# Values of the next batch moved into the delta rule's substitution, buffers laid out anew, slices in another order

## What is computed

```python
x = L0_attn_x                                             # 8 x 512 x 128
xn = layernorm(x)
x = x + L0_attn(xn) * silu(L0_ffn(xn))
xn = layernorm(x)
x = x + L1_attn(xn) * silu(L1_ffn(xn))

def L0_ffn(x):                       # 8 experts, the top 2 for each token
    h = silu(a) * g; weighted sum of the experts' outputs
def L0_attn(x, Wq, Wk, Wv, Wo):      # 16 heads, keys of 8, values of 64
    v = (x @ Wv).reshape(B, T, HEADS, D_V).transpose(0, 2, 1, 3)
    attn = softmax(where(causal, -inf, q @ k.T / scale))
    return (attn @ v) @ Wo
def L1_attn(hidden):                 # 4 heads of 32: delta rule in chunks of 32
    q, k, v = silu(causal conv(hidden @ W))
    attn = -strictly_lower(kb @ k.T)
    for i in range(1, c):            # the substitution: rows of the triangle, one after the other
        attn[..., i, :i] += attn[..., i, :] @ attn[..., :, :i]
    u, w = (attn + I) @ v, (attn + I) @ kb
    scan over chunks: u_new = u - w @ S; o = q @ S + lower(q @ k.T) @ u_new; S += k.T @ u_new
    mix o with an exponential average, normalise by its mean square, @ Wo
def L1_ffn(x):                       # two layers of windowed attention, then gelu gates
    x = x + local_attention(rotary(l2norm(q)), rotary(l2norm(k)), v) @ wo
    x = x + (a * gelu(g)) @ w2
```

## Time and profile before

| | us |
|---|---|
| median of 3 runs | 2367.35 |
| lowest and highest | 2362.2, 2369.82 |
| the profiled execution | 2383.33 |
| its span, first to last instruction | 2381.5 |
| busy in the span: PE, DVE, ACT, POOL | 1810.0, 1384.0, 1313.1, 537.8 |
| granted clock of PE, mean | 0.85 |

### The profile page before, as it was taken

The page is one execution under the profiler, slowest core; times in us unless marked ns, Lnnn a source line. Parts: engine busy times, 40 slices in busy tenths (PEclk is TensorE's granted clock), DMA queues, the critical chain, the costliest instruction groups (busy, mean ns, idle before and its releaser), DMA issues.

```text
span 2381.5 us, 54180 instructions
## 1 busy us (share of the span) xinstructions
PE 1810.0 (76%) x22372; PEld 1114.9 (47%) x22372; DVE 1384.0 (58%) x3033; ACT 1313.1 (55%) x3546; POOL 537.8 (23%) x597
## 2 busy tenths in 40 slices
PE   4587567886788676887778777986788686986877
PEld 3244234455454444455444544455444444455435
DVE  7633447375655647375755657474756657464653
ACT  1465337672576538662676448662676448661533
POOL 1222022130503022130503032120503032220330
PEclk9789677897789878897789877996889777996999
DMA  8323440003100200003100220003200220001000
GB/s 247 108 80 106 88 109 17 2 17 60 30 3 17 55 20 18 2 17 60 30 3 16 55 20 18 2 17 60 30 3 16 55 20 18 2 18 19 16 1 21
DMA packets 130210, 88.91 MB, mean 37 GB/s; under 512 B 75426, under 2 KB 120908, under 8 KB 126892
## 3 DMA queue, kind: packets, MB, share of 16 engines
q1 hardware_dynamic: 124332, 64.47, 11.4%
q10 hardware_dynamic: 2560, 14.68, 2.7%
q0 software_dynamic: 3072, 6.30, 2.2%
HBM read 41.77 MB, written 28.97 MB: 30 GB/s over the span
## 4 chain that ended last, share of the span: by engine, by line
PE 43%; ACT 19%; DVE 16%; issue 13%; POOL 6%; DMA 2%; SPq 1%; another core or an unknown queue 0%; DVEq 0%; POOLq 0%; ACTq 0%
ACT work_a L809 6%; PE PS L1318 4%; PE PS L599 4%; ACT area_b L1513 3%; PE PS L1396 3%; PE PS L1427 3%; POOL area_b L1698 3%; PE PS L1345 2%; ACT work_a L829 2%; PE PS L571 2%; PE PS L609 2%; PE PS L507 2%; PE PS L1438 2%; PE PS L755 2%; DVE work_a L947 2%
## 5 line engine op out<-in xcount | busy, mean ns | idle before, releaser
L809 ACT ACTIVATE work_a<-PS,work_a 128x512 bf16<-128x512 f32 (+3 forms) x512 | 266.8, 553 | 84.5 <-DVE work_a L947 80.8
L1698 POOL TENSOR_TENSOR area_b<-area_b,tables 128x256 f32<-128x256 f32 x256 | 207.9, 832 | 383.9 <-DVE area_b L1606 383.7
L947 DVE TENSOR_REDUCE work_a<-PS 128x2 f32<-128x1024 f32 (+3 forms) x256 | 200.1, 819 | 80.5 <-PE PS L484 76.6
L829 ACT ACTIVATE work_a<-PS 128x1024 f32<-128x1024 f32 (+1 forms) x192 | 169.5, 883 | 131.5 <-PE PS L484 128.8
L1513 ACT ACTIVATE area_b<-PS,neg_max 128x128 f32<-128x128 f32 x512 | 183.1, 388 | 38.5 <-DVE neg_max L1619 38.4
L1318 PE MATMUL PS<-wqkv,area_b 128*128 128x512 f32 x384 | 193.5, 636 | 7.2 <-DVE area_b L1606 6.5
L599 PE MATMUL PS<-work_a 128*64 128x512 f32 (+3 forms) x1024 | 183.1, 458 | 0.0
L1712 POOL TENSOR_TENSOR rstd_b<-var_eps_b,minus_half 128x4 f32<-128x4 f32 x16 | 16.4, 1027 | 667.0 <-DVE var_eps_b L119 667.0
L1345 PE MATMUL PS<-area_b 64*64 64x128 f32 (+1 forms) x2048 | 150.5, 293 | 17.8 <-ACT area_b L1513 12.0
L537 PE MATMUL PS<-work_a 64*128 64x512 bf16 (+3 forms) x512 | 82.6, 368 | 84.4 <-ACT work_a L809 75.1
L1345 PEld LDWEIGHTS PS<-area_b 64*64 64x64 f32 x2048 | 121.0, 148 | 51.9 <-issue 26.6
(11 more groups left out here) (310 smaller groups left out, 4161.8 us busy)
## 6 DMA issues: line engine op xcount, KB each, us to landing
work_a<-stack_d SPq DMA_DIRECT2D x32, 512.0 KB, 8.9
stack_d<-area_b SPq DMA_DIRECT2D x48, 192.0 KB, 3.1
v_back<-area_b ACTq DMA_DIRECT2D x16, 512.0 KB, 5.7
v_back<-area_b ACTq DMA_DIRECT2D x16, 384.0 KB, 3.7
stack_d<-area_b SPq DMA_DIRECT2D x32, 128.0 KB, 2.6
area_b<-in_L_attn_x_dram SPq DMA_DIRECT2D x4, 512.0 KB, 6.7
stack_d<-work_a SPq DMA_DIRECT2D x4, 512.0 KB, 7.2
work_a<-xnT_d SPq DMA_DIRECT2D x8, 256.0 KB, 3.2
```

The costliest lines, as they stand in the source:

```text
L809: nc.scalar.activation(dump0[:, n % 2 * T:n % 2 * T + (i + 1) * P], PS[:, a:a + (i + 1) * P], ACT.Exp, bias=neg_max0[:, k:k + 1], accum_ou ...
L829: nc.scalar.activation(probsT[:, a:a + 2 * n].rearrange("p (e c) -> p e c", e=2), PS[:, 0:1024].rearrange("p (e c) -> p e c", e=2)[:, :, 0 ...
L947: nc.vector.reduce_max(neg_max0[:, 2 * g * NT + i:(2 * g + 2) * NT:NT], at[:, :, Q_AT[i]:Q_AT[i] + (i + 1) * P], AX_X, negate=True).then_i ...
L1698: nc.gpsimd.tensor_tensor(to[:, n, :, r, :], src[:, n, :, 1 - r, :], table(2 * n + 1, t)[:, 32 * r:32 * r + 32].unsqueeze(1).to_broadcast( ...
```

## The change

Values of batch 0 are made where they were. Those of batch b+1 are now made inside batch b's delta rule, in the slices of the substitution: PE's four pairs of products go to banks 2 and 3, then 0 and 1, and so on by turns; ACT copies both halves in one instruction of 128x1024; DVE has no part in it. To have v0 free at that time the first stream's working buffer is laid out anew: v0 now lies over parts of the delta rule's buffers that are done with by then, xnT_b has a place of its own, and some small buffers share. PE waits for the load `xT` of the next batch and for the last of the `low` copies before the first pair, and for the last copy before `product`. The table ORDER is a new one on all five engines.

```diff
+        def values(k, t):
+            for half in range(2):
+                nc.tensor.matmul(bank(k + half), xnT_b[:, t * P:(t + 1) * P], wv0[:, half * 512:(half + 1) * 512],
+                                 start=True, stop=True).then_inc(sa["v"], 1)
 def attention_pe(pe, b):
-            pe.wait_ge(sa["xT"], ofa("xT", 16))
+                pe.wait_ge(sa["xT"], 16)
             for t in range(NT):
-                for half in range(2):
+                if b == 0:
                     if t:
-                        pe.wait_ge(sa[("v_act", "v_dve")[half]], ofa("v_act", t))
-                    nc.tensor.matmul(bank(2 + half), xnT_b[:, t * P:(t + 1) * P], wv0[:, half * 512:(half + 1) * 512],
-                                     start=True, stop=True).then_inc(sa["v"], 1)
+                        pe.wait_ge(sa["v_act"], t)
+                        pe.wait_ge(sa["v_dve"], t)
+                    values(2, t)
                 yield
...
 def delta_pe(pe, b):
...
+            after = counted(A_COUNTS, b + 1)
             for n in range(SUB_SLICES + 1):
-                yield
+                t = n - 1
+                if b + 1 < B and 0 <= t < NT:
+                    if t == 0:
+                        pe.wait_ge(sa["xT"], after("xT", 16))
+                        pe.wait_ge(sd["low"], ofd("low", 8))
+                    if t >= 2:
+                        pe.wait_ge(sa["v_act"], after("v_act", t - 1))
+                    values((2, 0)[t % 2], t)
+                yield
+            if b + 1 < B:
+                pe.wait_ge(sa["v_act"], after("v_act", NT))
             pe.wait_ge(sd["level"], ofd("level", 1))
...
 def delta_act(act, b):
...
             for n in range(SUB_SLICES + 1):
+                t = n - 1
+                if b + 1 < B and 0 <= t < NT:
+                    k = (2, 0)[t % 2]
+                    act.wait_ge(sa["v"], after("v", 2 * t + 2))
+                    nc.scalar.copy(v0[:, 2 * t * T:2 * (t + 1) * T], PS[:, k * BANK:(k + 2) * BANK]
+                                   ).then_inc(sa["v_act"], 1)
                 yield
...
         ORDER = {
             "tensor":
-                "H13 A6 H1 A13 H1 A1 H2 A1 H1 A1 H2 A1 H1 A1 H2 A1 H1 A1 H5 A2 H1 A1 H2 A9 H1 A1 H4 A1 H1 A3 H1 A8 H1 A1 "
+                "H13 A3 H1 A4 H3 A1 H1 A5 H1 A10 H2 A1 H2 A1 H1 A1 H2 A2 H3 A1 H2 A1 H1 A6 H1 A1 H3 A1 H1 A9 H1 A1 H1 A3 "
```

More of the change, by code:

```diff
@@ L309, in network @@
         take = taker(work_a, 17920)
-        v0 = take(NT * H0 * DV0)
         ctx0T = take(G0 * T)
@@ L323, in network @@
         zeros = take_head(T)
-        qS = take(G0 * T, BF16)
-        kS = take(G0 * T, BF16)
         probsT = take(3 * 1024)
-        xnT_b = probsT[:, 2560:3072]
         row_is = probsT[:, 0:2048].bitcast(BF16)
@@ L330, in network @@
         x_b = take(T)
-        dump0 = take(2 * T, BF16)
         neg_max0 = take(H0 * NT)
@@ L340, in network @@
         weight_b = take(2 * NT)
+        AT_VALUES = G0 * T + 3 * 1024 + 2 * T + 4 * H0 * NT + H0 * NT // 2 + 3 * H0 * NT + T + 4 * NT
+        v0 = take(NT * H0 * DV0)
+        qS = take(G0 * T, BF16)
+        kS = take(G0 * T, BF16)
+        xnT_b = take(T)
+        dump0 = xnT_b.bitcast(BF16)
         take = taker(work_a, 17920)
@@ L345, in network @@
         level = take(T)
+        stepT = level
         product = take(T)
-        qk_n = take(2 * T)
-        scaled = take(2 * T)
+        diff = product
         ema = take(T)
@@ L352, in network @@
         inv_t = take(2 * T)
+        mn = inv_t
+        uw = take(2 * T)
+        read_out = take(T)
+        tri_terms = read_out[:, 0:SUB * SUB // 4]
+        state = take(T)
+        tri, tri_inv = state[:, 0:SUB * SUB], state[:, SUB * SUB:2 * SUB * SUB]
+        take(AT_VALUES - 17 * T)
+        qk_n = take(2 * T)
+        scaled = take(2 * T)
+        take(NT * H0 * DV0 - 3 * T)
         conv = take(3 * T)
@@ L524, in attention_pe @@
                     pe.wait_ge(sa["stacked"], ofa("stacked", 64))
-                if m == 1:
-                    pe.wait_ge(sa["v_act"], ofa("v_act", NT))
-                    pe.wait_ge(sa["v_dve"], ofa("v_dve", NT))
+                if m == 1 and b == 0:
+                    pe.wait_ge(sa["v_act"], NT)
+                    pe.wait_ge(sa["v_dve"], NT)
                 if m >= 2:
@@ L779, in attention_act @@
             for t in range(NT):
-                act.wait_ge(sa["v"], ofa("v", 2 * t + 1))
-                nc.scalar.copy(v0[:, 2 * t * T:(2 * t + 1) * T], bank(2)).then_inc(sa["v_act"], 1)
+                if b == 0:
+                    act.wait_ge(sa["v"], 2 * t + 1)
+                    nc.scalar.copy(v0[:, 2 * t * T:(2 * t + 1) * T], bank(2)).then_inc(sa["v_act"], 1)
                 yield
@@ L922, in attention_dve @@
             for t in range(NT):
-                dve.wait_ge(sa["v"], ofa("v", 2 * t + 2))
-                nc.vector.tensor_copy(v0[:, (2 * t + 1) * T:(2 * t + 2) * T], bank(3)).then_inc(sa["v_dve"], 1)
+                if b == 0:
+                    dve.wait_ge(sa["v"], 2 * t + 2)
+                    nc.vector.tensor_copy(v0[:, (2 * t + 1) * T:(2 * t + 2) * T], bank(3)).then_inc(sa["v_dve"], 1)
                 yield
```

9 lines of the change are left out of this document (removed), and 157 rows, old and new, of the table ORDER.

## The result

| kernel | median, us | runs | ratio to the kernel before, 95% interval |
|---|---|---|---|
| before | 2366.35 (2362.2 to 2369.82) | 4 | |
| changed | 2412.27 (2400.2 to 2417.11) | 4 | 1.0180 [1.0157, 1.0204] |

The change makes the kernel 46 us slower. 2333 was forecast, and the range ended at 2368.

A forecast was written before the change was run, and what follows sets the result against it. Chains passing between engines were taken to bound the kernel, no engine filling a period. Front 4.6 plus substitution and tail 0.4 us, over seven periods, gave 35 us off; scaled to the runs' median, 2333 us, range 2296 to 2368.

The forecast's parts named there:

- the front: Start of each period, where the values' products and copies go: 4.6 us off per period, bounds 2.4 and 9.38.
- the forecast's 3: Substitution and tail of a period together: 0.4 us off per period, over seven periods.
- the substitution: Values' pairs move into PE's holes there: push of 0 to 2 us in most periods, 3.2 in one.
- The clock at the front: First q, k, v products fall into PE's slow stretch: L1318 some 1.9 us longer, a third charged, 0.6.
- DVE as the bound of the front: Front: DVE starts up to 2.96 us earlier and does 2.7 us less; 5.7 us upper value if it stays bound.
- wait for the landing: Substitution, one period: first pair waits for `xT` until 1350.3, making a context product 5.1 us late.
- its input comes with `inv_in`, unchanged: Substitution: L684's input taken as not delayed, so L684 starts near 1369.0 instead of 1365.80.
- The tail: End of a period, L692 and L702 moved ahead: 2.3 us back before L731 where nothing was pushed, bound 4.1.
- Rival 1: Stall at the substitution with pairs at the slower clock level: 5.1 us lost a period, 2403 us; chance 0.14.
- L1403's chain: Substitution, rival 1's path: L1403 15.8 us late at worst, 13.8 after its slack.
- Rival 2: Front gives almost nothing, ACT's stretch after 1177 taking back DVE's saving: 1 us a period left, 2360; chance 0.16.
- Rival 3: More gain: pairs fill PE's holes, clock stays up, L1396 gives 1.47 back; 10 us a period, 2298; chance 0.18.

The follow-up runs named there:

- e3: Changed kernel with the order of before in slices 12 to 65 of each batch on PE, ACT, DVE and POOL; 2405.08 us, ratio 1.0162.
- e1: Changed code under the order of before, except slices 66 to 71 on PE and ACT as in the changed kernel; 2403.67 us, ratio 1.0150.
- f4: Kernel before, with POOL's gathers behind the rotary products and the gathered rows used later, as in f3; 2364.14 us, ratio 0.9988.
- e7: e1 with both edits, e5's filler and e6's values behind the contexts; 2371.93 us, ratio 1.0013.
- e4: Changed kernel with the four pairs of values moved later on PE, and ACT's copies behind them; 2412.12 us, ratio 1.0183.
- e2: Code of before under the changed order, slices 0 to 25 and 76 to 92 on PE, ACT, DVE kept old; 2390.63 us, ratio 1.0111.
- e6: e1 with the pairs of values moved behind the last context products on PE; 2383.84 us, ratio 1.0063.
- f2: Kernel before with the changed order only in slices 12 to 53, on PE, ACT, DVE and POOL; 2395.03 us, ratio 1.0116.
- f3: e10 with the gathered rows used five score units later still, so DVE doesn't wait for them; 2356.88 us, ratio 0.9971.
- e5: e1 with four pairs of unread products put on PE where L507 stood, no copies; 2395.11 us, ratio 1.0121.
- e8: e7 with POOL's gathers moved behind the second stream's rotary products, their use four score units later; 2431.09 us, ratio 1.0258.
- e10: e6 with the gathers moved as in e8, so without the unread products; 2421.8 us, ratio 1.0217.

## Why the prediction was wrong

Against a forecast of 35 us less, the seven periods of the changed kernel's profile are 19 us longer, 54 us apart. By the table, 32 of these are the front (0.2 where 7 x 4.6 less was forecast), and 19 are loop 0 and the two stretches behind it, which the forecast left alone. From loop 1 to L731 the sum is 1 us less, near the forecast's 3, but that is luck: with slices 12 to 65 at their old places (e3) it is 24 us more, so the earlier `kk` hides a loss there. The failed steps are the front, the substitution and the order.

**The clock at the front: a term mis-sized.** The prediction saw that L1318 would fall into the slow stretch and charged 0.6 us for the first set. In e1 the later sets lost too (4.71 for 3.14 in the third, 4.78 for 4.02 in the fourth), since PE no longer had L507 between them. e1's front was 10.8 us longer over seven periods, and filler took 10.2 of it back. In the changed kernel the third set starts 0.5 us earlier and takes 1.1 us longer.

**DVE as the bound of the front: the step that failed.** "If DVE stays the bound" gave 2.96 + 2.7 = 5.7 us. The first half was right as an event: L1599 starts 2.7 us earlier. The rest was wrong: with the clock held up by filler, four copies fewer on DVE brought nothing (0.6). Products, reductions, rotary steps and turned products pass each tile around PE, ACT, DVE and POOL, and POOL, which the prediction left out of the front, could not start before its gathers were through: 12.0 us after `mixed`, before and after. A busy share of 9.79 on DVE didn't show that POOL's path was as long. Taking away only the gathers (f4, -0.5) or only the copies, with the clock held up (e7, 0.1), does not shorten the front; with both out of the way the gain appears: -16.7 us, 2.4 a period. That is half of what was forecast, and only with another edit.

**The substitution: the right wait, and a follower left out.** PE waited 4.96 us for `xT` in the changed kernel and 5.84 in e1, in the period where the working has it wait for the landing. But "its input comes with `inv_in`, unchanged" was wrong: DVE's queue holds context copies in the middle of the substitution, and these wait for PE. The prediction named who is queued behind the values on PE, not who is queued behind those on DVE. It cost 25.2 us in e1, 4.0 when the pairs stood behind the contexts. That the pairs' own time is nearly covered was right. In the changed kernel the wait was not the loss (e4), but the stretch to L684 is 11 us longer there than in e2; why stays open. The Trainium skill's rule ("DMA: Bandwidth & Descriptors", Rules for kernel authors) to wait for a transfer late pointed to this loss, and e1 against e6 agrees (25.2 and 4.0).

**The order: not costed.** The prediction read the new table at the start and at the end of a period and took the middle as alike. It wasn't: e2, the new order from slice 26 on, costs 24 us, and f2, slices 12 to 53 alone, 28. In the changed kernel it is the 19 us from loop 0 to q, k, v, against which it hides the loss in the substitution (e3).

**The tail** came out near its number, the stretch from L684 to L731 being 3.7 us shorter over seven periods. That isn't clear of what executions differ by there, and e3, with the same new order in the tail, is 7.7 longer, so the reason given for it isn't shown.

**The rivals.** Rival 1 had the sign and a near time (2403 for 2412), by the stall. For the changed kernel that was luck: with the stall away (e4) it is as slow. In e1 the stall is 25 of the 31 us by which the periods grew, but spread over five periods, and it came through DVE's queue rather than L1403's chain. Rival 2 had the front right, which gave nothing, but not the reason: ACT's stretch behind it did not take the gain back in f3, whose loop 0 is as before (-0.2). Rival 3's part on L1396 came true (3.73 for 6.67); what it gave isn't shown, as no run has it alone.

## What to carry to other kernels

When work leaves an engine, ask what it was doing for the others besides its own result: here products kept PE's clock up, and covered another engine's gathers. What the clock is worth depends on what else holds the stretch: the same filler gave 10 us at one front (e5) and cost 10 at another (e8 against e10). An engine that is busy all the time can share its place with another path of the same length, and then each must go before the time does. When a wait is added to a queue, follow it through the second queue as well: who waits behind the waiting instruction, and what stands behind that one. And a table of order that is new everywhere is a change of its own: test it with the old code before the code's effect is read from it.

## What the runs showed of the hardware

Eight products a period that nobody reads (e5 against e1) made the front 10.2 us shorter in seven periods, by the granted clock: 1.00 instead of 0.83 in the window shown, 2.84 instead of 4.71 us for the third set there. With POOL's gathers out of the way the same products made it 10 us longer (e8 against e10). An indirect gather held POOL for 1.3 us from one issue to the next (1138.67 to 1148.93 for eight), though DMA does the moving. And the prologue of one and the same kernel differed by 9.3 us between two executions (333.7 and 324.4).
